# State space sublayer: gate's projection ahead of the loop, engine orders changed, squares folded by GpSimd

## What is computed

```python
proj = x @ Win.T
x_ssm, z, Bm, Cm, dt_raw = split(proj)           # z: 32 heads x 64, the gate
dt = softplus(dt_raw + dt_bias)
xc, Bc, Cc = (silu(causal_conv(u, w)) for u, w in ...)   # 4 taps
decay = exp(dt * -exp(A_log))
# h = decay * h + (dt * xc) B;  y = h C, step by step over 128 tokens
y = y * rsqrt(mean(y * y, axis=-1) + 1e-6)       # per head
y = y * silu(z)
return y.reshape(B, T, H * P) @ Wout.T
```

## Time and profile before

| | |
|---|---|
| median of 3 runs | 2154.83 us (2151.45 to 2156.3) |
| profiled execution | 2158.32 us, its span 2156.5 us |
| TensorE, matmul | 1645.3 us busy (76%) |
| VectorE | 1434.9 us (67%) |
| ScalarE | 728.7 us (34%) |
| GpSimd | 476.9 us (22%) |
| mean granted TensorE clock | 0.854 |
| HBM read | 44.43 MB, 21 GB/s over the span |

### The profile page before, as it was taken

One profiled execution on the slowest core, in us unless ns is written; L12 is line 12 of the kernel. 1 busy time (PEld: TensorE's weight loads), 2 busy tenths in 40 slices (PEclk: granted clock), 3 DMA queues, 4 the chain that ended last, 5 costly groups with the idle time before them and its releaser, 6 DMA issues. The chain is left out here.

```text
span 2156.5 us, 32415 instructions
## 1 busy us (share of the span) xinstructions
PE 1645.3 (76%) x11633; PEld 1226.8 (57%) x11662; DVE 1434.9 (67%) x2376; ACT 728.7 (34%) x1143; POOL 476.9 (22%) x549
## 2 busy tenths in 40 slices
PE   2799999998886888166747458889995988888353
PEld 2687888887773564022446234677764875556221
DVE  3588777877225754899576673554446993677977
ACT  0466556665221441233224111333331002345111
POOL 0233323332000421277112002210001322143000
PEclk9899999999897786588869667999996997999555
DMA  2000000000000000000100002000002210100000
GB/s 106 25 24 21 29 29 29 28 16 23 0 0 21 2 7 32 0 0 0 42 3 2 25 0 100 2 19 1 1 1 64 73 39 27 51 4 2 1 0 20
DMA packets 13206, 46.80 MB, mean 22 GB/s; under 512 B 1715, under 2 KB 2356, under 8 KB 11830
## 3 DMA queue, kind: packets, MB, share of 16 engines
q1 hardware_dynamic: 13110, 45.49, 6.1%
HBM read 44.43 MB, written 1.05 MB: 21 GB/s over the span
## 5 line engine op out<-in xcount | busy, mean ns | idle before, releaser
L2024 DVE SCALAR_TENSOR_TENSOR arena<-psum,arena 128x1016 f32<-128x1016 f32 (+2 forms) x240 | 303.9, 1267 | 100.2 <-ACT arena L1960 94.5
L859 DVE TENSOR_REDUCE limits<-psum 128x4 f32<-128x512 f32 (+2 forms) x256 | 148.3, 620 | 95.2 <-PE psum L719 59.0
L1855 PE MATMUL psum<-ssm_XT_hi,ssm_split 128*128 128x512 f32 x640 | 196.0, 409 | 17.3 <-POOL ssm_split L1813 10.9
L827 ACT ACTIVATE PT<-psum 128x1024 f32<-128x1024 f32 x112 | 108.6, 1021 | 120.5 <-PE psum L750 120.5
L719 PE MATMUL psum<-K,QR 32*128 32x256 f32 (+1 forms) x320 | 125.0, 475 | 26.6 <-POOL K L695 16.4
L1960 ACT ACTIVATE arena<-psum,arena 128x1024 f32<-128x1024 f32 x80 | 89.0, 1112 | 158.3 <-PE psum L1855 158.3
L1855 PEld LDWEIGHTS psum<-ssm_XT_hi,ssm_split 128*128 128x128 f32 x640 | 117.4, 193 | 39.5 <-POOL ssm_split L1813 14.0
L2370 PE MATMUL psum<-expert,x 128*128 128x256 f16 x1024 | 114.7, 277 | 16.8 <-POOL expert L2356 16.8
L1812 POOL TENSOR_TENSOR ssm_split<-arena,const 128x256 fp32r<-128x256 f32 x80 | 58.4, 730 | 291.0 <-DMA arena<-in_ssm_in 164.3
L2508 POOL TENSOR_TENSOR fed<-dtx,b_all 128x1024 f32<-128x1024 f32 x32 | 103.1, 3243 | 77.8 <-ACT b_all L2557 44.3
L2370 PEld LDWEIGHTS psum<-expert,x 128*128 128x128 f16 x1024 | 101.5, 99 | 29.8 <-issue 16.9
(11 more groups left out here) (415 smaller groups left out, 3691.9 us busy)
## 6 DMA issues: line engine op xcount, KB each, us to landing
arena<-in_ssm_in SPq DMA_DIRECT2D x32, 384.0 KB, 3.1
expert_mask<-in_expert_masks SPq DMA_DIRECT2D x32, 256.0 KB, 2.6
arena<-in_L_xattn SPq DMA_DIRECT2D x1, 5120.0 KB, 15.1
arena<-in_L_ffn SPq DMA_DIRECT2D x1, 2592.0 KB, 9.1
arena<-in_L_xattn SPq DMA_DIRECT2D x2, 1280.0 KB, 5.4
arena<-in_L_attn SPq DMA_DIRECT2D x1, 2272.0 KB
arena<-in_L_ffn SPq DMA_DIRECT2D x1, 2176.0 KB, 8.5
arena<-in_L_xattn SPq DMA_DIRECT2D x1, 1667.0 KB, 6.8
```

The costliest lines, as they stand in the source:

```text
L827: nc.scalar.activation(PT[:, u % 2, 2 * k:2 * k + 2, :, :].rearrange("p r h q -> p (r h q)"), p.psum[:, (2 + 2 * k) * 512:(4 + 2 * k) * 51 ...
L859: ins = nc.vector.tensor_reduce(limits[:, u % 2, r, :, k], score_bank(r)[:, :].rearrange("p (h k) -> p h k", h=4)[:, :, lo:hi], AX.X, ALU. ...
L1855: ins = nc.tensor.matmul(bank[tile_bank(r, tile) + half][:, :], w_part(tile, kw, c), x_part(kx, c, slice(half * 512, (half + 1) * 512)), s ...
L2024: ins = nc.vector.scalar_tensor_tensor(out[:, :, ago:], product[:, :, :P - ago], tap, out[:, :, ago:], ALU.mult, ALU.add)
```

## The change

1. The gate's projection leaves the loop. In the block in front SyncE loads all gate weights (4 groups of 512 KB, into the part of `gated` that is written last), GpSimd splits each group in two fp32r parts, TensorE projects 32 pieces (4 groups x 8 sequences) with three fp32r products each, 6 matmuls of 512 columns, and ScalarE writes SiLU of each piece to `gated`. 16 pieces stand ahead of the cumulative sums, 16 behind. The split of X^T moves to the block's start (its high part to ScalarE).
2. In the loop TensorE, ScalarE and VectorE get new orders. On VectorE mixes 0 and 1 stand ahead of convolutions 1 and 2, mixes 2 and 3 behind them; each weighing of turned tokens stands right ahead of convolution 3 and 4 (tiles counted from 0). `product_bank` uses banks 5, 6, 7, 6, and `products` waits only at group 3.
3. GpSimd folds the 64 squares of a head twice (to 32, to 16) behind the gating multiply; VectorE then sums 16.
4. The second load of a pair leaves the gate's part out and waits for the split of tile 4 instead of the gate's projection.

```diff
@@ def ssm_weights
-    return np.concatenate([tiles, z], axis=2).reshape(n, DC, P, 2, 3 * P).transpose(0, 3, 2, 1, 4)
+    tiles = np.concatenate([tiles, np.zeros_like(z)], axis=2).reshape(n, DC, P, 2, 3 * P).transpose(0, 3, 2, 1, 4)
+    return tiles, wz.T.reshape(DC, P, 4, 4 * P).transpose(2, 1, 0, 3)
@@ block in front
                 def _(sync):
+                    for g in range(4):
+                        sync.dma_start(z_raw[g].rearrange("p (c n) -> p c n", c=DC), p.dram["ssm_z"][g]).then_inc(s.loaded.up(16), 16)
                     p.load_next(sync)
+                @block.gpsimd
+                def _(pool):
...
+                    for g in range(4):
+                        if g == 0:
+                            pool.wait_ge(s.loaded.sem, s.loaded.at(63))
+                        if g >= 2:
+                            pool.wait_ge(s.z_psum.sem, s.z_psum.at(8 * (g - 2) + 7))
...
+                        p.pool_chain.then(pool, nc.gpsimd.tensor_tensor(hi.rearrange("p (o n) -> p o n", n=P), z_raw[g].rearrange("p (o n) -> p o n", n=P), ones8, ALU.mult))
+                        nc.gpsimd.tensor_tensor(lo, z_raw[g], hi.bitcast(F32), ALU.subtract).then_inc(s.split_ready.up(), 1)
                 @block.tensor
+                    def project_z(g, b):
...
+                        if n >= 4:
+                            pe.wait_ge(s.z_ready.sem, s.z_ready.at(n - 4))
+                        products = [(kw, kx, c) for kw, kx in ((0, 0), (0, 1), (1, 0)) for c in range(DC)]
+                        for kw, kx, c in products:
+                            ins = nc.tensor.matmul(z_bank(n)[:, :], (XT_hi, XT_lo)[kx][:, c, b * P:(b + 1) * P],
+                                                   z_split[g % 2][kw][:, :].rearrange("p (c n) -> p c n", c=DC)[:, c, :],
...
+                    for n in range(16):
+                        project_z(n // 8, n % 8)
                     pe.wait_ge(s.dt_ready.sem, s.dt_ready.at(0))
...
+                    for n in range(16, 32):
+                        project_z(n // 8, n % 8)
                 @block.scalar
+                    for n in range(32):
...
+                        nc.scalar.activation(gated[:, 4 * g:4 * g + 4, b * P:(b + 1) * P], z_bank(n)[:, :].rearrange("p (k n) -> p k n", k=4), ACT.Silu
+                                             ).then_inc(s.z_ready.up(), 1)
@@ loop block, sync
-                                sync.wait_ge(s.z_psum.sem, s.z_psum.at(m + -1))
+                                sync.wait_ge(s.split_ready.sem, s.split_ready.at(m * TILES + -1))
@@ loop block, gpsimd
+                            pool.wait_ge(s.square_ready.sem, s.square_ready.at(m + -1))
+                            by_head = square[:, :].rearrange("p (k n) -> p k n", n=64)
+                            p.pool_chain.then(pool, nc.gpsimd.tensor_tensor(by_head[:, :, :32], by_head[:, :, :32], by_head[:, :, 32:], ALU.add))
+                            nc.gpsimd.tensor_tensor(by_head[:, :, :16], by_head[:, :, :16], by_head[:, :, 16:32], ALU.add).then_inc(s.sums_ready.up(trips), 1)
@@ loop block, tensor
                             products(0)
-                            pe.wait_ge(weights_here[1].sem, weights_here[1].at(m * 16 + -1))
-                            project_z()
-                            outputs(0)
                             products(1)
                         if has_a:
                             project(m, r, 2)
                         if has_b:
+                            outputs(0)
                             outputs(1)
-
-                            pe.wait_ge(s.z_ready.sem, s.z_ready.at(m + -1))
                             products(2)
+                            products(3)
                         if has_a:
-                            pe.wait_ge(s.conv_silu.sem, s.conv_silu.at(m * TILES))
-                            turn_x(0)
                             project(m, r, 3)
                         if has_b:
                             outputs(2)
-                            products(3)
+                            outputs(3)
                         if has_a:
+                            pe.wait_ge(s.conv_silu.sem, s.conv_silu.at(m * TILES))
+                            turn_x(0)
+                            project(m, r, 4)
                             pe.wait_ge(s.dtx_ready.sem, s.dtx_ready.at(m * 2))
                             turn_x(1)
-                            project(m, r, 4)
-                        if has_b:
-                            outputs(3)
@@ loop block, scalar
                             tap(m, r, 1)
...
+                            tap(m, r, 2)
                             silu(m, r, 1)
-                            tap(m, r, 2)
+                            silu(m, r, 2)
                             tap(m, r, 3)
-                            silu(m, r, 2)
-                            tap(m, r, 4)
-                            silu(m, r, 3)
                         if has_b:
...
                             nc.scalar.activation(square[:, :], p.psum[:, 4 * 512:6 * 512], ACT.Square).then_inc(s.square_ready.up(trips), 1)
+                        if has_a:
+                            silu(m, r, 3)
+                            tap(m, r, 4)
@@ loop block, vector
                             mix(0)
+                            mix(1)
                         if has_a:
                             convolve(m, r, 1)
-                        if has_b:
-                            mix(1)
-                        if has_a:
                             convolve(m, r, 2)
                         if has_b:
                             mix(2)
+                            mix(3)
...
-                            dve.wait_ge(s.square_ready.sem, s.square_ready.at(m + -1))
+                            dve.wait_ge(s.sums_ready.sem, s.sums_ready.at(m + -1))
```

More of the change, by code:

```diff
@@ L1683, in state_space @@
             dtx = spare(2, B, P)
-            bc = [[spare(T) if (r, k) == (1, 3) else sb2(f"bc{r}{k}", [P, T])[:, :] for k in range(TILES - 1)] for r in range(2)]
+            early = [sb2(f"bc0{k}", [P, T])[:, :] for k in range(2)]
+            late = spare(T)
             XT_hi = sb2("XT_hi", [P, DC, T], F32R)
@@ L1701, in state_space @@
             assert taken[0] <= ARENA[1]
-            with nc.Block(no_gpsimd_drain=True) as block:
+            with ExitStack() as first, nc.Block(no_gpsimd_drain=True) as block:
+                z_split = [[first.enter_context(nc.sbuf_tensor(f"ssm_z{r}{k}", [P, T], F32R)) for k in range(2)] for r in range(2)]
                 row = lambda t: t.rearrange("p (o n) -> p o n", o=1).broadcast_to([P, B, SSM_H])
+                z_raw = [gated[:, 12 + g, :] for g in range(4)]
+                z_bank = lambda n: bank[4 + n % 4]
@@ L1709, in _ @@
                 @block.tensor
                 def _(pe):
+                    def project_z(g, b):
+                        n = 8 * g + b
+                        if b == 0:
+                            pe.wait_ge(s.split_ready.sem, s.split_ready.at(g))
+                        if n == 0:
+                            pe.wait_ge(s.x_ready.sem, s.x_ready.at(1))
+                        if n >= 4:
[4 more added lines that the diff above has]
+                                                   z_split[g % 2][kw][:, :].rearrange("p (c n) -> p c n", c=DC)[:, c, :],
+                                                   start=(kw, kx, c) == products[0], stop=(kw, kx, c) == products[-1])
+                        ins.then_inc(s.z_psum.up(), 1)
@@ L1757, in state_space @@
             p.close()
+            bc = [early + [sb2(f"bc0{k}", [P, T])[:, :] for k in (2, 3)], [sb2(f"bc1{k}", [P, T])[:, :] for k in range(3)] + [late]]
             def steps(engine, emit, chain=None, links=0):
@@ L1837, in state_space @@
                 decay_bank = lambda g: bank[4 + g]
-                product_bank = lambda g: bank[5] if g < 2 else bank[6]
+                product_bank = lambda g: bank[(5, 6, 7, 6)[g]]
                 @block.tensor
@@ L1871, in decay_sums @@
                             ins.then_inc(s.decay_psum.up(trips), 1)
[L1873 to L1879 removed]
                         def products(g):
                             n = m * 4 + (g - 4)
[L1884 removed]
+                            if g == 3:
+                                pe.wait_ge(s.mixed_ready.sem, s.mixed_ready.at(n + -2))
                             for q in range(4):
@@ L2063, in step @@
                             convolve(m, r, 3)
-                        if has_b:
-                            mix(3)
-                        if has_a:
                             weigh_x(1)
```

46 lines of the change are left out of this document (20 added, 26 removed).

## The result

The changed kernel takes **2179.43 us** (median of 4 runs, 2178.02 to 2180.14), the one before 2153.14 us on the same chip (4 runs, 2149.77 to 2156.3): ratio 1.0122, 95% interval 1.0104 to 1.014. The change costs 1.2%. The prediction was 2181 us, in a range of 2167 to 2197.

A forecast was written before the change was run, and what follows sets the result against it. The prediction took TensorE's queue to set the loop's turn of 29.85 us. Front +39.7, loop -11.3 and ends -2.0 summed to +26.4 us, giving 2181 us against the median, in a range of 2167 to 2197.

The forecast's parts named there:

- The forecast case: Main case: a chain of waits ties the loop at 29.1 us a turn, front costs 39.7 us; chance 0.77.
- Part 1, the chain: Loop without the gate's projection: waits through VectorE, TensorE and ScalarE sum to a turn of 29.1 us.
- The saving per turn: In the loop: 0.75 us less than 29.85 a turn, over fifteen turns 11.3 us.
- Edits at nothing: Loop edits costed at zero: GpSimd's folds, VectorE's shorter sum, the earlier smaller load, products losing waits.
- Part 2, the ends: First and last steps of the loop: -1.3, +0.7, -3.9 and +2.5, together -2.0 us.
- Part 3, the front: Block ahead of the loop: gate loads, splits and projection delay the loop's first load from 50.79 to 90.5, +39.7 us.
- The sum: Whole kernel: front 39.7, loop -11.3 and ends -2.0 give +26.4 us.
- TensorE stays the bound: Rival in the loop: turn falls to 26.3 us, loop gains 54 us, time 2139 us; chance 0.06.
- The clock falls: Rival in the loop: TensorE's pauses lower its clock, doubling 2.4 us a turn, time 2217 us; chance 0.07.
- GpSimd becomes late: Rival in the loop: late folds push convolution 1 back some 0.6 us a turn, time 2190 us; chance 0.10.

The follow-up runs named there:

- experiment 4: The changed kernel without GpSimd's two folds, VectorE summing 64 squares per head again; 2182.55 us, ratio 1.0133.
- experiment 11: Changed kernel with tap 4 before SiLU 3, tap 1 before SiLU 0, first turning behind projection 3, no folds, products awaiting only their own exponential; 2106.16 us.
- experiment 2: Changed kernel with tap 4 ahead of SiLU 3, tap 1 ahead of SiLU 0, first turning right behind projection 3; 2128.2 us, ratio 0.9874.
- experiment 8: Changed kernel in which GpSimd starts splitting the gate's weights only when VectorE's step sizes are ready; 2182.11 us in a single run.
- experiment 3: Kernel before with only the gate's projection moved to the front, keeping its orders, banks and sum of 64 squares; 2188.9 us, ratio 1.0166.
- experiment 7: The changed kernel with one move only, tap 1 ahead of SiLU 0 and the second table load; 2166.71 us, ratio 1.0047.

## Why the prediction was right

The forecast case came: a chain ties the loop, the front is paid in full. Point by point, by the steps of the prediction:

- **Part 1, the chain.** Right link by link. In the rows above: convolutions 1 and 2 7.57 (308.13 to 315.70), mix to outputs 0.73, outputs to turning 1.84 (forecast 1.77), turning to weighing 0.73 (0.65), weighing 0.61, convolution 3 until ScalarE 3.89, SiLU and tap 2.10, convolution 4 3.91, SiLU 4 to SiLU 0 5.75 (300.28 to 306.03), SiLU 0 and tap 1 2.10. Sum 29.23, forecast 29.1. TensorE's waits were forecast at 1.6 and 1.6, and are 1.46 and 1.44. The two table loads are there, each right behind its neighbour and 1.28 long. So the trace does not bear out the drain that the Trainium skill (ScalarE: Activation LUTs, What ACT_TABLE_LOAD costs) adds to each switch: its turn of 31.9 did not come.
- **The saving per turn** was 0.59 over fourteen equal turns, 8.3 us, where I had 0.75 over fifteen, 11.3.
- **Edits at nothing.** The folds were right in time (they end at 327.7, the sum is due at 329.39, so 1.7 us of cover where I had 2). But that the shorter sum is worth nothing was **wrong**: experiment 4 prices it at 0.57 us a turn, nearly all that the turn gained (0.59). My reason, that the convolution of tile 0 (convolution 1 in the prediction, which counts from 1) ends before the exponentials do, with some 1 us of room, holds with the short sum only, by 0.24 us: it ends at 304.35 and, as experiment 4 shows (338.47 to 338.62), takes 0.15 to reach ScalarE, which comes free at 304.74. The 0.8 us of the longer sum less these 0.24 are the 0.57. I took the chain's length for the changed kernel as it is, so its sum came out nearly right, and the credit went to the wrong edit: that is luck.
- **Part 2, the ends.** Mis-sized: -2.0 forecast, -6.9 measured. From products 0 to the copy it is 9.35 us (567.91 to 577.26) against 15.6, 6.2 less where I had 3.9, because only products 0 and 1 ran at the low clock (2.05 us for 8 records at 567.91), which cost some 1.7 us and not 4; behind the copy 2.7 more (forecast 2.5); the first turns gained 3.0, of which I had 0.6. With the turns: -15.2 against -13.3.
- **Part 3, the front.** +37.1 against +39.7. Loads landed at 33.77 (34.3), TensorE started at 38.68 (39.1), the low clock cost 1.8 instead of 3 (the first ten matmuls took 4.09 us, where ten take 2.33 later), and a matmul took 0.2325 us instead of 0.2375.
- **The sum** was +26.4, and the spans differ by 21.2: 5.2 too much. The final 2181 lies nearer to 2179.43 than that, since the 3.5 us that I took off because the profiled execution of before lay above its median had no counterpart after: that one took 2179.51, on its median. Two errors cancelled in part. That the two medians differ by 26.3 us, just the sum, is luck too: by the profiles front and loop give 21.9 of it, and the other 4.4 are no effect that the prediction named.

**The rivals.** *TensorE stays the bound* did not hold, but experiment 11 is that case made true, with 24.8 a turn and not the 26.3 that I gave. I had taken 3.57 from the turn with its waits; taken from TensorE's work alone (29.83 - 1.5 of waits - 3.57) it is 24.8, and just that was measured. *The clock falls*: 1.00 in the loop, with pauses of 1.46 and 1.44 us, so not here. The trace of the changed kernel shows the gaps without the loss, that of experiment 4 shows both, below. *GpSimd becomes late* did not hold in the changed kernel, came in experiment 2 with 1.14 us, and cost nothing there.

## What to carry to other kernels

Taking work off the busiest engine pays only as far as the next chain of waits is shorter: walk that chain link by link with measured durations before and after, and treat each wait in the code as written (all four exponentials, not the one that is needed). The wait that stands in the trace ahead of an instruction was about the most that one reordering in front of it won here (waits of 0.57, 1.53 and 2.02 us, gains of 0.67, 1.65 and 1.70; the wait of 1.14 in experiment 2 won nothing), and single gains don't add: of these moves two brought 1.65 and 1.7 alone and 1.8 together, while a third grew from 0.67 to 1.6. When a hoist looks like a loss, price the orders in the loop before giving up on it; here five small edits (three moves, no folds, one wait split) turned 1.2% slower into 2.4% faster.

## What the runs showed of the hardware

**VectorE slowed threefold by GpSimd.** Nine chained operations of 128x256, both inputs in SBUF, took 4.10 us in the kernel before, 12.28 in the changed one, where GpSimd splits the gate's weights beside them, and 4.10 again in experiment 8, where the splits wait. VectorE's timelines, before, changed, experiment 8:

```profile
34.99 4.10 DVE L2637 SCALAR_TENSOR_TENSOR arena<-arena 128x256 f32<-128x256 f32 x9
```

```profile
33.05 12.28 DVE L2670 SCALAR_TENSOR_TENSOR arena<-arena 128x256 f32<-128x256 f32 x9
```

```profile
35.07 4.10 DVE L2671 SCALAR_TENSOR_TENSOR arena<-arena 128x256 f32<-128x256 f32 x9
```

The convolutions read PSUM and one input in SBUF, and they did not suffer: 3.87 us for three at 325.60, with GpSimd folding beside them, and 3.86 at 300.49. The Trainium skill (SBUF — State Buffer, SBUF: two separate sides) states just this difference: a VectorE operation with two inputs in SBUF and a GpSimd operation that reads SBUF exclude each other, for a whole instruction. The trace agrees: the operation that starts at 33.97 in the changed kernel took 2.45 us, as long as one of GpSimd's (2.37 and 2.41), where nine of them take 4.10 undisturbed. In the prediction I had put these chains down as hidden without counting on this. They stayed hidden, since TensorE wanted the step sizes only behind its first 16 pieces.

**A clock lost after a wait of 1.10 us, and not after 1.46.** In experiment 4 TensorE waited 1.10 us for a mix, and from there on records took up to twice as long; the granted clock was 0.50 of full speed, the lower of its two levels, in the third row (windows of 2 us), and it was back at 1.00 from 296 on:

```profile
288.00:290.00 2.00, 0.90 (x6) 0.44 (x4) 2.00 (x3) 0.80 (x1) 1.11 (x2) 1.00 0.00 0
290.00:292.00 2.00, 2.00 (x17) 2.00 (x18) 0.36 (x1) 1.26 (x2) 0.35 (x1) 0.87 0.00 0
292.00:294.00 2.00, 2.00 (x9) 1.71 (x8) 0.99 (x2) 1.86 (x2) 0.00 (x0) 0.50 0.00 0
```

Thirty microseconds later, after the same wait, 1.02 us long (320.20), the clock fell again (0.55 from 322 to 324 us), and so it did after 200.43 (in a turn that stayed at 29.78) and 439.65; after the same waits at 260.02 (1.03 us) and 350.32 (1.10) it stayed at 1.00, and so it did in the full turns of the changed kernel, with waits of 1.46 and 1.44. In experiment 3 it fell in every third turn, after waits of 1.66 to 1.71 us, and not after equal ones between (1.68 at 316.45). So the length of the wait does not decide it; what does stays open. The mean clock of the whole program does not tell such losses: it is 0.850 in experiments 3 and 4, and 0.849 in experiment 7, whose full turns all ran without one. Windows of a few microseconds do.
